# Unit 0's row maxima moved from the start of attention into the last stretch of the projection stage

## The chip, the cores and the metric

The kernel runs on one core of one Trainium2 chip. The metric is the device time of one execution in microseconds; the median of several runs is compared. In the notes below PE is TensorE, DVE is VectorE, ACT is ScalarE, POOL is GpSimd and SP is the queue that issues most DMAs.

## The reference, cut to what matters

```python
# x: (4, 2048, 256); 16 heads of 16; window 128 on each side; key 0 and query 0 see everything
x = x + attention(layernorm(x)) @ Wo.T
x = x + ffn(layernorm(x))

logits  = einsum('bhqd,bhkd->bhqk', q, k) * SCALE
logits  = where(|i - j| <= 128 or i == 0 or j == 0, logits, -inf)
out     = softmax(logits) @ v

# ffn: both matrices ternary, with one scale for each row
h = x @ (tern(w_fc) * scale).T + gate * (x @ v.T @ fast_b.T @ u.T)
y = relu(h)**2 @ (tern(w_proj) * scale).T
```

## The kernel before

The work is in three stages, each with its instructions written out for every engine; semaphores tie the engines together. A stage ends for all engines at the end of its block: the next block's first instructions start together.

**Projection** (`stage_project`). Sixteen groups of 512 rows of x are normalised, turned and multiplied into q, k and v. q and k are split into three bf16 parts (HIGH, MID, LOW; `q_parts`, `k_parts`) and stored to DRAM, v (`va`) too. ACT writes HIGH and MID, DVE the rests, POOL the LOW parts (L448). Beside that DVE prepares the weights of the third stage in small pieces, `weights.dve_part(dve, i)`, two pieces for each group; making one 128x256 piece of a matrix ternary is a pair of instructions, L1027 and L1029 (`dve_ternary`), both with two operands in SBUF.

**The projection's tail.** When the sixteenth group is through, the row of query 0, which sees all keys, is computed. The maximum over the keys is taken on DVE (L716), turned on PE (L573), reduced again and put on a diagonal (L804, L806), spread over the partitions by a product (L576, the tensor `over_bank`), added to the scores (L809, the tensor `w0`), put through Exp on ACT (L681), and multiplied with v on PE: 16 rounds n of four products (L581, one for each sequence, each in its own 32 output rows). DVE divides and picks (L817, L819), PE gathers (L585), DVE copies the row out (L823), and SP, after it has waited for all q, k and v stores (L411, L412), stores the row (L414). On DVE the rest of the weights' work lies between L809 and L817: `dve_low` and five ternary pairs.

**Attention** (`stage_attend`). 64 units (16 groups of 512 queries, times four sets of four heads) pass through a pipeline, written as steps: in step i unit i-2 has its maxima taken (L_MAX), unit i-3 has them turned and split (L_SHIFT), unit i-4 has its scores and Exp (L_SCORE), unit i-5 its sums with v. For the maxima PE makes 16 tiles of 128 queries by up to 387 keys (L1503) into four PSUM banks, DVE reads each with a mask and a maximum (L1665); PE then turns the maxima (L1483, "M"), ACT, DVE and POOL split them (L1612, L1654, L1627, L1409), SP writes them as extra rows of q, and the scores (L1527) have them subtracted. In the first steps the engines also set up what attention needs: POOL writes an identity, a gate and three 32x4128 areas of ones (L1262); ACT writes the fourth (L1593) and copies the turned weights out of PSUM (`act_w1`, `act_u`, `act_w2`); PE turns them between the tiles of unit 0; and before unit 0's scores ACT clears the score banks (L1639, semaphore `s_init`), behind unit 0's Exp at key 0 (L1631), which needs POOL's L1414. POOL's L1409 and L1414 stand behind its three areas of ones.

**Feed forward** (`stage_feed`) follows and is not touched.

The wait at the head of unit 0's scores is this:

```python
if n == 0:
    if us.n == 0:
        pe.wait_ge(s_init, 3)
    if us.n < UPG:
        pe.wait_ge(s_ones[us.hq], 1)
    pe.wait_ge(s_row[us.upar], (us.uhalf + 1) * DMA * SHIFT_ROWS)
```

## Time and profile before

| what | value |
|---|---|
| median of 3 runs | 1153.87 us (1153.65 to 1155.17) |
| profiled execution, its time | 1157.08 us |
| its span in the profile | 1155.4 us |
| granted TensorE clock, mean | 0.992 |
| PE, DVE, ACT, POOL busy | 98%, 85%, 73%, 61% of the span |
| projection with its tail | 0 to 185.05 us |
| attention | 185.05 to 781 us, the last of its sums (L1549) |
| feed forward | the rest |

The rows give a start in microseconds from the span's beginning and a duration. A row with "x8" merges eight instructions of one kind. What stands in brackets is how long the engine sat idle ahead of it and what ended that. One fp32 product appears as two records. The span is 1.7 us shorter than the profiled execution's time, and that execution was 3.2 us above the median.

### The profile page before, as it was taken

The page shows a single profiled execution, that of the slowest core. Times are in us where ns is not written, and L with a number is a line of the kernel's source. Part 1 is how long each engine was busy: PE and PEld are TensorE (multiplying, and loading weights), DVE is VectorE, ACT ScalarE, POOL GpSimd, SP SyncE. Part 2 cuts the span into 40 slices and gives each one's busy share as a digit, 9 for nine tenths or more (in the row PEclk, how much of TensorE's full clock was granted, in tenths as well). Part 3 has the DMA queues.
Part 4 walks back from the last instruction along what each step waited for, and adds up shares of the span by engine and source line. Part 5 has one row for each costly group of instructions (what it writes and reads, how often), then busy time and mean ns, then how long its engine had stood idle before and what let it go on. Part 6 is the DMA issues. An engine that isn't in the chain of part 4 may idle for free.

```text
span 1155.4 us, 26575 instructions
## 1 busy us (share of the span) xinstructions
PE 1126.5 (98%) x9115; PEld 784.2 (68%) x9115; DVE 978.4 (85%) x3169; ACT 843.7 (73%) x1513; POOL 706.7 (61%) x935
## 2 busy tenths in 40 slices
PE   8999998999999999999999999999999999999997
PEld 7888884455555555555555555558888988898886
DVE  7789857899889998899888999867888888888885
ACT  7989984788888878888888888875565556555654
POOL 3665565577788777887778877773344334433443
PEclk9999998899999999999999999999999999999999
DMA  6999997655556556555565464240231113111201
GB/s 196 287 296 276 268 235 187 120 123 130 129 132 130 129 119 139 131 119 131 129 137 132 112 138 109 69 139 28 73 107 59 56 55 107 59 55 56 74 20 37
DMA packets 158150, 145.24 MB, mean 126 GB/s; under 512 B 21548, under 2 KB 157760, under 8 KB 158016
## 3 DMA queue, kind: packets, MB, share of 16 engines
q1 hardware_dynamic: 158016, 143.54, 49.5%
q8 instruction: 73, 1.20, 0.5%
q14 instruction: 61, 0.50, 0.2%
HBM read 91.74 MB, written 50.95 MB: 124 GB/s over the span
## 4 chain that ended last, share of the span: by engine, by line
PE 72%; DVE 7%; issue 2%; ACT 1%; POOL 1%; DVEq 0%; POOLq 0%; ACTq 0%
PE e_psum L1549 15%; PE e_psum L1503 15%; PE e_psum L1527 14%; PE e_psum L1837 6%; PE e_psum L1839 5%; PE e_psum L1267 3%; PE e_psum L1818 3%; PE e_psum L1817 3%; DVE n_stats L142 2%; DVE f_x L1936 2%; PE e_psum L1822 1%; PE e_psum L255 1%; PE e_psum L254 1%; PE e_psum L253 1%; PE e_psum L1786 1%
## 5 line engine op out<-in xcount | busy, mean ns | idle before, releaser
L1665 DVE CUSTOM_DVE_ANT_0 a_masked<-e_psum,band 128x387 f32<-128x387 f32 (+1 forms) x1024 | 493.2, 534 | 59.3 <-PE e_psum L1503 56.4
L1622 ACT ACTIVATE a_weights<-e_psum 128x1024 f32<-128x1024 f32 (+1 forms) x512 | 397.9, 806 | 87.2 <-PE e_psum L1527 82.3
L1401 POOL TENSOR_SCALAR_AFFINE_SELECT a_weights<-a_weights 128x1024 f32<-128x1024 f32 x256 | 276.2, 1091 | 59.9 <-ACT a_weights L1622 58.7
L1503 PE MATMUL e_psum<-e_k,e_q 96*128 96x387 bf16 (+1 forms) x1024 | 281.2, 326 | 3.5 <-PEq L281 2.0
L1878 POOL TENSOR_TENSOR f_square<-f_relu 128x512 f32<-128x512 f32 x128 | 146.1, 1142 | 209.6 <-ACT f_relu L1867 192.2
L1527 PE MATMUL e_psum<-e_q,e_k 128*128 128x384 bf16 (+2 forms) x1408 | 255.5, 278 | 1.5 <-ACT a_weights L1622 1.1
L1549 PE MATMUL e_psum<-a_weights,a_v 128*17 128x384 f32 (+2 forms) x2816 | 195.8, 392 | 1.0 <-POOL a_weights L1401 1.0
L1527 PEld LDWEIGHTS e_psum<-e_q,e_k 128*128 128x128 bf16 x1408 | 128.9, 98 | 95.7 <-issue 39.7
L1503 PEld LDWEIGHTS e_psum<-e_k,e_q 96*128 96x128 bf16 x1024 | 100.3, 98 | 99.8 <-DVE a_max L1665 44.6
L1837 PE MATMUL e_psum<-w_w_t,f_square_hi 128*128 128x256 f32 x512 | 129.4, 287 | 5.6 <-DVE f_square_lo L1924 5.6
L1839 PE MATMUL e_psum<-w_w_t,f_square_lo 128*128 128x256 f32 x512 | 126.7, 282 | 0.0
L1867 ACT ACTIVATE f_relu<-e_psum,w_mag 128x512 f32<-128x512 f32 x128 | 87.2, 681 | 52.7 <-PE e_psum L1822 52.7
L1924 DVE TENSOR_TENSOR f_square_lo<-f_square,f_square_hi 128x512 fp32r<-128x512 f32 x128 | 98.5, 789 | 24.2 <-POOL f_square L1878 24.2
L1549 PEld LDWEIGHTS e_psum<-a_weights,a_v 128*17 128x17 f32 x2816 | 61.6, 96 | 67.5 <-issue 53.7
L1837 PEld LDWEIGHTS e_psum<-w_w_t,f_square_hi 128*128 128x128 f32 x512 | 96.6, 189 | 15.1 <-DVE f_square_lo L1924 12.1
L1817 PE MATMUL e_psum<-f_xt_hi,w_w_t 128*128 128x512 f32 x256 | 102.7, 401 | 1.1 <-ACT f_relu L1867 1.1
L1818 PE MATMUL e_psum<-f_xt_lo,w_w_t 128*128 128x512 f32 x256 | 101.2, 395 | 0.0
L1839 PEld LDWEIGHTS e_psum<-w_w_t,f_square_lo 128*128 128x128 f32 x512 | 96.9, 189 | 2.9
L1870 ACT ACTIVATE f_square_hi<-f_relu 128x512 fp32r<-128x512 f32 x128 | 81.0, 633 | 4.1
L448 POOL TENSOR_TENSOR p_q_parts<-p_rest,p_q_parts 128x512 bf16<-128x512 f32 x32 | 38.3, 1196 | 71.2 <-ACT p_q_parts L613 71.2
L1665 DVE DVE_READ_ACCUMULATOR2_ANT a_max<- 128x1 f32 x1024 | 78.8, 77 | 0.0
L1860 ACT ACTIVATE f_z<-e_psum 128x512 fp32r<-128x512 f32 x16 | 9.6, 597 | 90.1 <-PE e_psum L1809 90.1
(217 smaller groups left out, 2057.0 us busy)
## 6 DMA issues: line engine op xcount, KB each, us to landing
k_parts<-p_k_parts SPq DMA_DIRECT2D x48, 258.0 KB, 5.2
e_k<-k_parts SPq DMA_DIRECT2D x64, 193.5 KB, 3.8
e_k<-k_parts SPq DMA_DIRECT2D x192, 64.5 KB, 3.4
q_parts<-p_q_parts SPq DMA_DIRECT2D x48, 256.0 KB, 5.7
e_q<-q_parts SPq DMA_DIRECT2D x64, 192.0 KB, 3.9
e_q<-q_parts SPq DMA_DIRECT2D x192, 64.0 KB, 3.4
v_ones<-p_va SPq DMA_DIRECT2D x16, 544.0 KB, 6.4
p_x<-in_x SPq DMA_DIRECT2D x16, 512.0 KB, 7.4
```

The source lines that it names most:

```text
L1401: pool.affine_select(out=blocks, in_=blocks, compare_op=ALU.is_ge, fill=0.0, base=0, pattern=[[0, NQ // 2 * HEAD_COLS // P // CUT_STEP], [ ...
L1503: pe.matmul(sh.tile_bank(ux, j)[:, lo:hi], qw[ux.q][0:SLOT_ROWS, h, t * P:t * P + P], kt[ux.hq][0:SLOT_ROWS, h, start + lo:start + hi], st ...
L1527: ins = pe.matmul(score[third // 2][:, c0:c0 + m * P], kt[us.hq][:, h, k0:k0 + P], qw[us.q][:, h, qb * P:(qb + m) * P], start=True, stop=True)
L1549: ins = pe.matmul(sum_bank[32 * j:32 * j + VW, qb * P:(qb + m) * P], vw[:, up.gpar, kb + 1, h * VW:h * VW + VW], pe_w[:, up.upar, c0:c0 + ...
L1622: act.activation(pe_w[:, us.upar, lo:hi], score[c % 2][:], ACT.Exp).then_inc(s_exp, 1)
L1665: dve.tensor_tensor_reduce(out=masked[:, ux.upar, h, t:t + hi - lo], in0=bank[:, lo:hi], in1=band[:, lo:hi], scale=1.0, scalar=NEG, op0=AL ...
L1817: pe.matmul(self.h_bank[j % 2][:], lhs, self.sh.xt_hi[:, q.par, k, :], start=(k == 0), stop=False)
L1818: pe.matmul(self.h_bank[j % 2][:], lhs, self.sh.xt_lo[:, q.par, k, :], start=False, stop=False)
L1837: pe.matmul(y, sh.r2_hi[:, j % 4, part], self.w.w2_t[:, j, :], start=(j == 0 and t == 0), stop=False, skip_group_check=True)
L1839: ins = pe.matmul(y, sh.r2_lo[:, j % 4, part], self.w.w2_t[:, j, :], start=False, stop=(j == MH - 1), skip_group_check=True)
L1878: pool.tensor_tensor(sh.r2[:, j % 4, :], sh.r[:, j % 4, :], sh.r[:, j % 4, :], ALU.mult).then_inc(self.s_sq, 1)
L1924: dve.tensor_tensor(sh.r2_lo[:, j % 4, :], sh.r2[:, j % 4, :], sh.r2_hi[:, j % 4, :].bitcast(F32), ALU.subtract).then_inc(self.s_r2lo, 1)
```

## The change

- `sh.pe_first_tile` and `sh.dve_first_tile`: the 16 tiles and maxima of unit 0 are made in the projection's tail. They use three banks in turn. On PE tiles 0 and 1 stand behind L576, tiles 2 to 4 behind the wait for `w0`, and tiles 5 to 15 one each between the rounds of query 0's sums. On DVE tile 0 stands ahead of `w0`, the others behind it. The masked values are written over the q parts of the even groups, so DVE waits for their stores.
- `dve_part`: all eight ternary pairs of `w_proj` now stand in the last three groups (three, three and two, where there was one each), the filling of `v_t` in an earlier group; the five pairs in the tail are gone.
- ACT issues the loads of q of units 2 and 3 in the tail, behind Exp; SP no longer issues them in attention (their k it still does).
- Attention begins with the maxima of unit 1. The turning of the weights on PE stands between unit 1's tiles, and ACT's first copies stand behind unit 0's MID. The identity is kept from the first stage; POOL no longer writes it again.
- POOL writes the mask band (`pool_band`) in group 5 and not in the tail.

```diff
@@ stage_project, SP
             sp.wait_ge(s_v, G * TB)
-            for n in range(1, PRELOADED):
-                sh.load_unit(sp, Unit(n), q_dram, k_dram)
+            sh.load_unit(sp, Unit(1), q_dram, k_dram)
@@ stage_project, POOL
+                    if q.g == GB + 1:
+                        sh.pool_band(pool)
 
             sweep(body, LP)
-            sh.pool_band(pool)
-            pool.wait_ge(sh.s_band, 2)
             pool.wait_ge(s_v, G * TB)
+            pool.wait_ge(s_gap, G * KT)
             sh.pool_zeros(pool)
@@ stage_project, PE
             pe.matmul(over_bank[:, 0:B * H], ones[0:B * H, :], m_diag[:], start=True, stop=True).then_inc(s_rpe, 1)
-            idle_products(total_bank, 10)
+
+            sh.pe_first_tile(pe, 0)
+            sh.pe_first_tile(pe, 1)
+            idle_products(sum_bank, 4)
+            pe.wait_ge(s_rv, 4)
+            for j in range(2, 5):
+                sh.pe_first_tile(pe, j)
             pe.wait_ge(s_rexp, 1)
             for n in range(NB):
                 for b in range(B):
                     ins = pe.matmul(sum_bank[QR * b:QR * b + H, 0:VROW], w0[:, b, n, :], v_of[:, b, n, 0:VROW],
                                     start=(n == 0), stop=(n == NB - 1))
+                if n + 5 < TILES:
+                    sh.pe_first_tile(pe, n + 5)
             ins.then_inc(s_rpe, 1)
@@ stage_project, ACT
+
+            act.wait_ge(s_v, G * TB)
+            for n in range(PRELOADED, Q_PRELOADED):
+                sh.load_q(act, Unit(n), q_dram)
@@ stage_project, DVE
+            dve.wait_ge(s_qout[0], DMA * STORES * (G // 2))
+            sh.dve_first_tile(dve, 0, masked)
             dve.wait_ge(s_rpe, 2)
             for b in range(B):
                 ins = dve.tensor_tensor(w0[:, b], s0_of[:, b],
                                         over_bank[:, b * H:(b + 1) * H].unsqueeze(1).broadcast_to([P, NB, H]), ALU.add)
             ins.then_inc(s_rv, 1)
+            for j in range(1, TILES):
+                sh.dve_first_tile(dve, j, masked)
             weights.dve_low(dve)
-            for n in range((2 * G - weights.TERN2) // 2, 4 * KT):
-                weights.dve_ternary2(dve, n)
+            dve.wait_ge(sh.s_tile_read, TILES)
+            dve.tensor_copy(sh.first_key0[:].rearrange("p (c r) -> p r c", r=3), masked[:, :, 0:TILES // 3 + 1])
             dve.wait_ge(s_rpe, 3)
@@ Weights.dve_part
-        elif i >= self.TERN2 and i % 2 == 0:
-            self.dve_ternary2(dve, (i - self.TERN2) // 2)
+        elif i >= self.TERN2:
+
+            for n in ((0, 1), (2,), (3, 4), (5,), (6,), (7,))[i - self.TERN2]:
+                self.dve_ternary2(dve, n)
@@ Shared
+    def pe_first_tile(self, pe, j):
+
+        if j == 0:
+            pe.wait_ge(self.s_load[0], self.loaded(Unit(0)))
+        if j >= 3:
+            pe.wait_ge(self.s_tile_read, j - 2)
+        t, h = divmod(j, NQ)
+        start, lo, hi = self.keys_of(0, t)
+        pe.matmul(self.first_bank(j)[:, lo:hi], self.qw[0][0:SLOT_ROWS, h, t * P:t * P + P],
+                  self.kt[0][0:SLOT_ROWS, h, start + lo:start + hi], start=True, stop=True).then_inc(self.s_tile, 1)
@@ stage_attend, SP
                 if (u := at(0)) and u.n >= PRELOADED:
                     wait(sp, s_score, (u.n - Q_BUFS) * CHUNKS + CHUNKS)
-                    sh.load_unit(sp, u, q_dram, k_dram)
+                    sh.load_k(sp, u, k_dram)
+                    if u.n >= Q_PRELOADED:
+                        sh.load_q(sp, u, q_dram)
@@ stage_attend, POOL
-            identity(pool, ident[:], s_ident)
@@ stage_attend, PE
-                    if not ux:
+                    if not ux or ux.n == 0:
                         return
...
-                    if ux and ux.n == 0 and j in (1, 3):
-                        pe.wait_ge(s_ident, 2)
+                    if ux and ux.n == 1 and j in (1, 3):
                         weights.pe_w1(pe, 2 + j // 2)
...
-                    if ux and ux.n == 1 and j == 3:
+                    if ux and ux.n == 1 and j == TILES - 1:
                         weights.pe_mag(pe)
```

In the tail of the projection, PE's rows before are these; L576 spreads the maxima, L487 are ten products that nobody reads, L581 are the sums of query 0, and attention begins behind the branches:

```order
L573 MATMUL p_bank<-p_ident,p_m_tok 64x128
L1077 MATMUL p_bank<-p_ident,z_w_in 128x128 x4
L576 MATMUL p_bank<-p_m_diag,p_ones 128x64
L487 MATMUL p_bank<-p_ones 128x128 x10
L581 MATMUL p_bank<-p_va,p_w 16x272 x64
L585 MATMUL p_bank<-p_picked,p_seq_of 4x272
L281 UNCONDITIONAL_BRANCH
L1457 UNCONDITIONAL_BRANCH
L1503 MATMUL e_psum<-e_k,e_q 128x258 x2
```

And these are PE's rows there now; L580 is the old L576, L1297 is `pe_first_tile`, and L591 is the old L581:

```order
L580 MATMUL p_bank<-p_m_diag,p_ones 128x64
L1297 MATMUL e_psum<-e_k,e_q 128x258 x2
L491 MATMUL p_bank<-p_ones 128x128 x4
L1297 MATMUL e_psum<-e_k,e_q 128x258 x2
L1297 MATMUL e_psum<-e_k,e_q 128x387
L591 MATMUL p_bank<-p_va,p_w 16x272 x4
L1297 MATMUL e_psum<-e_k,e_q 128x387
L591 MATMUL p_bank<-p_va,p_w 16x272 x4
L1297 MATMUL e_psum<-e_k,e_q 128x387
...
L1297 MATMUL e_psum<-e_k,e_q 128x387
L591 MATMUL p_bank<-p_va,p_w 16x272 x20
L597 MATMUL p_bank<-p_picked,p_seq_of 4x272
```

Where 64 products of the sums stood in one piece, eleven tiles now stand between the first eleven rounds of four; the last five rounds follow in one piece.

On DVE, the last group of the projection and what follows it before the change, from the last ternary pair of the group (L1027, L1029) to `w0` (L809):

```order
L733 TENSOR_TENSOR p_rest<-p_bank,p_k_parts 128x512 x2
L1027 TENSOR_TENSOR z_below<-z_w_in,z_nhalf 128x256
L1029 SCALAR_TENSOR_TENSOR z_w_in<-z_w_in,z_half,z_below 128x256
L716 TENSOR_REDUCE p_m_tok<-p_va 128x16
L804 TENSOR_REDUCE p_m_neg<-p_bank 64x1
L806 TENSOR_SCALAR p_m_diag<-p_ident,p_m_neg 64x64
L809 TENSOR_TENSOR p_w<-p_va,p_bank 128x256 x4
```

And the same place now, where L732 is the maximum over the keys, L1307 is `dve_first_tile` and L828 is `w0`:

```order
L1054 TENSOR_TENSOR z_below<-z_w_in,z_nhalf 128x256
L1056 SCALAR_TENSOR_TENSOR z_w_in<-z_w_in,z_half,z_below 128x256
L1054 TENSOR_TENSOR z_below<-z_w_in,z_nhalf 128x256
L1056 SCALAR_TENSOR_TENSOR z_w_in<-z_w_in,z_half,z_below 128x256
L732 TENSOR_REDUCE p_m_tok<-p_va 128x16
L820 TENSOR_REDUCE p_m_neg<-p_bank 64x1
L822 TENSOR_SCALAR p_m_diag<-ident,p_m_neg 64x64
L1307 ISA p_q_parts,first_max<-e_psum,band 128x258
L1307 ISA first_max 128x1
L828 TENSOR_TENSOR p_w<-p_va,p_bank 128x256 x4
```

A second ternary pair stands ahead of the maximum over the keys, and unit 0's first tile ahead of `w0`.

On POOL, the start of attention before, with its four small setup instructions and the three areas of ones, ahead of the LOW split of unit 0's maxima:

```order
L106 MEMSET e_ident 128x128
L108 AFFINE_SELECT e_ident<-e_ident 128x128
L1385 MEMSET a_gate 128x16
L1387 AFFINE_SELECT a_gate<-a_gate 128x16
L1262 MEMSET e_k 32x4128 x3
L1409 TENSOR_TENSOR a_shift<-a_neg_rest,a_shift 16x128
L1414 TENSOR_TENSOR a_d<-a_masked,a_max 128x16
```

And now:

```order
L1448 MEMSET a_gate 128x16
L1450 AFFINE_SELECT a_gate<-a_gate 128x16
L1326 MEMSET e_k 32x4128 x3
L1472 TENSOR_TENSOR a_shift<-a_neg_rest,a_shift 16x128
L1477 TENSOR_TENSOR a_d<-first_key,first_max 128x16
```

The identity is gone from the head; the areas of ones still stand between the block's start and unit 0's LOW.

## Rows read from the trace of the kernel before

**Rows 1.** The page's costliest groups: busy us, mean ns of one | idle before, releaser.

```profile
L1665 DVE CUSTOM_DVE_ANT_0 a_masked<-e_psum,band 128x387 f32<-128x387 f32 (+1 forms) x1024 | 493.2, 534 | 59.3 <-PE e_psum L1503 56.4
```

**Rows 2.** Windows of 25.6 us: busy time by engine, clock, DMA share, GB/s.

```profile
179.20:204.80 25.60, 19.08 (x126) 11.48 (x119) 18.51 (x76) 11.42 (x17) 11.87 (x9) 0.82 0.76 168
```

**Rows 3.** The final chain, 150 to 260 us: start, duration, what.

```profile
194.35 0.29 PE e_psum L1483
...
203.66 0.38 PE e_psum L1483
```

**Rows 4.** Timeline of the projection's tail: start, duration, engine, line, operands.

```profile
168.88 0.61 DVE L716 TENSOR_REDUCE p_m_tok<-p_va 128x16 f32<-128x256 f32 x1 [1.43 <-ACT p_va L618]
...
170.34 0.64 DVE L806 TENSOR_SCALAR p_m_diag<-p_ident,p_m_neg 64x64 f32<-64x64 f32 x1
...
171.03 0.43 PE L576 MATMUL p_bank<-p_m_diag,p_ones 64*128 64x64 f32 x2 [0.61 <-DVE p_m_diag L806]
...
171.50 1.41 DVE L809 TENSOR_TENSOR p_w<-p_va,p_bank 128x256 f32<-128x256 f32 x4 [0.53 <-PE p_bank L576]
...
174.06 7.53 PE L581 MATMUL p_bank<-p_va,p_w 128*16 128x272 f32 x128 [0.16 <-ACT p_w L681]
...
175.60 0.68 DVE L1051 TENSOR_TENSOR w_wo_lo<-p_bank,w_wo_hi 128x512 fp32r<-128x512 f32 x1
...
183.14 0.41 DVE L823 COPY row<-p_bank 4x256 f32<-4x256 f32 x1 [0.71 <-PE p_bank L585]
...
184.25 0.26 SPq L414 DMA_DIRECT2D attention<-row  x1
185.05 0.55 SPq L1228 DMA_DIRECT2D e_k<-k_parts  x1
```

**Rows 5.** Timeline of the first steps of attention.

```profile
185.56 0.11 POOL L1385 MEMSET a_gate<- 128x16 f32 x1
...
186.02 10.50 POOL L1262 MEMSET e_k<- 32x4128 f32 x3
...
193.24 0.60 ACT L1122 ACTIVATE w_w_t<-e_psum 128x512 fp32r<-128x512 f32 x1 [0.34 <-PE e_psum L1094]
...
198.12 2.06 ACT L1639 ACTIVATE e_psum<-e_ident 128x1024 f32<-128x1024 f32 x3
...
203.83 1.06 PE L1527 MATMUL e_psum<-e_q,e_k 128*128 128x384 bf16 x4
```

**Rows 6.** Timeline of DVE and POOL, a ternary pair and LOW parts in two groups.

```profile
130.37 0.89 DVE L1027 TENSOR_TENSOR z_below<-z_w_in,z_nhalf 128x256 f32<-128x256 f32 x1
130.94 1.31 POOL L448 TENSOR_TENSOR p_k_parts<-p_rest,p_k_parts 128x512 bf16<-128x512 f32 x1
131.30 1.24 DVE L1029 SCALAR_TENSOR_TENSOR z_w_in<-z_w_in,z_half,z_below 128x256 f32<-128x256 f32 x1
...
166.51 0.41 DVE L1027 TENSOR_TENSOR z_below<-z_w_in,z_nhalf 128x256 f32<-128x256 f32 x1
166.96 0.48 DVE L1029 SCALAR_TENSOR_TENSOR z_w_in<-z_w_in,z_half,z_below 128x256 f32<-128x256 f32 x1
...
168.44 1.12 POOL L448 TENSOR_TENSOR p_k_parts<-p_rest,p_k_parts 128x512 bf16<-128x512 f32 x1
```

**Rows 7.** The final chain in attention, sums between other products.

```profile
218.34 0.77 PE e_psum L1549 x8
219.10 0.27 PE e_psum L1503
...
219.60 0.17 PE e_psum L1503
```

**Rows 8.** DMA issues from 174 to 182 us, and a wait of SP.

```profile
v_ones<-p_va SPq DMA_DIRECT2D x1, 544.0 KB, 10.1
...
e_q<-q_parts SPq DMA_DIRECT2D x1, 192.0 KB, 7.0
...
SPq L412 <- DMA v_ones<-p_va: 0.9, 1, 0.9
```

More of the change, by code:

```diff
@@ L1132, with __init__ @@
 class Shared:
-    def __init__(self, nc, outer, ctx, row, band, weights_words):
+    def __init__(self, nc, outer, ctx, row, band, ident, first, weights_words):
         def sb(name, shape, dt=F32):
@@ L1148, in sem @@
             return outer.enter_context(nc.semaphore(f"e_{name}"))
-        self.nc, self.row, self.band = nc, row, band
+        self.nc, self.row, self.band, self.ident = nc, row, band, ident
+        self.first_key0, self.first_max = first
         with ExitStack() as place:
@@ L2067, in layer @@
         band = outer.enter_context(nc.sbuf_tensor("band", [P, -(-WINDOW // 16) * 16], BF16))
+        ident = outer.enter_context(nc.sbuf_tensor("ident", [P, P], F32))
+        first = [outer.enter_context(nc.sbuf_tensor(f"first_{name}", shape, F32))
+                 for name, shape in (("key0", [P, TILES + 2]), ("max", [P, TILES]))]
         with ExitStack() as place:
             weights = Weights(nc, outer, wo, fast_b, w_fc, w_proj, u, v, gate)
-            sh = Shared(nc, outer, place, row, band, Weights.WORDS)
+            sh = Shared(nc, outer, place, row, band, ident, first, Weights.WORDS)
         stage_project(nc, x, (wq, wk, wv), q_dram, k_dram, va_dram, o_dram, weights, sh)
```

105 lines of the change are left out of this document (65 added, 40 removed).

## The prediction

> **What bounds the kernel now.** The final chain runs through PE's products in nearly all of attention and feed forward, so work that is moved can give time back only where PE is not full. I read the windows for such a stretch: it is the seam between projection and attention: from 179.20 to 204.80 PE is busy for 19.08 of 25.6 us, at a granted clock of 0.82 of full speed [rows 2]. The seam has three pieces. The tail is a chain through DVE, PE and ACT from the maximum over the keys at 168.88 to the row's store at 184.25, with 7.53 us of sums on PE as its longest link [rows 4]. Attention starts at 185.05 [rows 4]. Its first unit's maxima are turned at 194.35 and the second's at 203.66 [rows 3]: each time 16 tiles that DVE reads at 0.53 us each [rows 1]. At 203.83 PE starts on unit 0's scores [rows 5], 18.78 us after attention began. The question is how much of these 18.78 us falls away, and what the tail pays for it.
>
> **What attention gives back.** The plain count is 194.35 - 185.05 = 9.3 us, all of unit 0's maxima [rows 3, 4]. But unit 0's scores wait for two things. The second is a chain that begins with the block on POOL: the gate's setup (185.56), three areas of ones (186.02, 10.50 us), then LOW and key 0's difference, then ACT's Exp, the weights' magnitudes and the clearing of the score banks (198.12, 2.06 us, so to 200.18) [rows 5]. Before the change it ends 3.65 us ahead of 203.83 and costs nothing. It stays in the new kernel, shorter by the identity only. The gate's first instruction will stand at the block's start, so the chain takes 200.18 - 185.56 = 14.62 us, and with 0.05 for PE to see it the scores start 14.7 us into attention. Gain: 18.78 - 14.7 = **4.1 us**, not 9.3. ACT's first copies, moved behind unit 0's MID, ended at 193.84, 8.8 us into the block [rows 5]; now they begin about 1.6 us later and end at about 10, beneath POOL's memsets. Unit 1's tiles with the weights between them take what unit 0's took, some 10 us, and are covered too; if that cover were gone, each microsecond past 14.7 would be paid. Unit 1's turned maxima and unit 2's first tile are then ready when the scores start. This, and a clock that may rise earlier than it did, I put at **0.3 us**, between 0 and 1.2.
>
> **What the tail pays.**
>
> *Ternary pairs.* Two stand where one stood in the last group. The first keeps its 166.51 and 166.96 and ends at 167.44 [rows 6]; but a pair that meets POOL's LOW parts took 0.89 and 1.24 us, with the 1.24 lasting beyond POOL's 1.31 [rows 6]. In the last group the second pair runs into LOW parts too, one of them at 168.44 [rows 6], so it costs 2.17 us (130.37 to 132.54 [rows 6]) to twice 1.24. I take 2.5: it ends at 169.95 and the maximum over the keys starts 1.07 us late. Some comes back at L806: its 0.64 us for 64x64 ended with a LOW part, which will be over by then; I estimate 0.3. PE's spreading product moves from 171.03 by **+0.8** (0 if the pairs don't meet, +2 if L806 meets the first memset of q's rows instead). The Trainium skill, "SBUF — State Buffer", section "SBUF: two separate sides", says that a DVE instruction with two SBUF inputs and a GpSimd instruction that reads SBUF exclude each other for whole instructions. By it the second pair can only run between two LOW parts, as the slow rows show; without it this term would be 0 and the total 0.8 us less. The pairs moved into the two groups before may make DVE's next rests a microsecond or two late, but the banks that these free are wanted by PE only a group later, and DVE catches up in its waits for ACT (1.43 us even in the last group [rows 4]): nothing is paid there. The filling of `v_t` is hidden likewise.
>
> *Tile 0 ahead of `w0`.* DVE now waits for one product more and reads one tile, 0.53 us [rows 1], less what it waited anyway: **+0.5**. Exp and the sums start 1.3 us late, at about 175.4.
>
> *Eleven tiles between the rounds.* 128 records of sums in 7.53 us [rows 4] are 16 rounds at 0.47, in which four products run at once in their own rows. A tile needs the whole array. The trace has this pattern in attention: eight records of 384 columns in 0.77 us, and the tile after them shows 0.27 where others show 0.17 [rows 7]. Together 0.87, where the tail's pace would give 384/272 x 0.47 = 0.66: breaking a piece costs 0.21. Each inserted tile so costs 0.17 + 0.21 = 0.38, eleven of them **+4.2**. The bounds are 11 x 0.17 = 1.9 (nothing for breaking) and 5.5 (0.5 each, were weight loads bare as well).
>
> *DVE's end.* Tile 15's product comes behind round 11, at 175.4 + 11 x 0.85 = 184.7, and is read by 185.5; then comes `dve_low`, which lay between 172.91 and 176.28, 3.4 us with the filling of `v_t` [rows 4]; I take 2.0 for what is left with the copy of key 0's column (1.5 to 3.4). DVE is ready at 187.5, PE's sums at 187.1: **+0.4**.
>
> *The end.* Before, the row's copy ended at 183.55, but SP stored it at 184.25 [rows 4], since it waited 0.9 us for the last store of v, which took 10.1 us to land [rows 8]. The new q loads on ACT's queue, 8 DMAs and 0.77 MB, share the same DMA engines; at the 168 GB/s of that window [rows 2] they delay that landing by at most 4.6 us, from 184.0 to 188.6. The copy now ends at 183.55 + 0.8 + 0.5 + 4.2 + 0.4 = 189.45, after it. So SP's wait is gone: **-0.6**.
>
> The tail grows by 0.8 + 0.5 + 4.2 + 0.4 - 0.6 = 5.3 us, and attention starts at about 190.35.
>
> **Sum.** +5.3 - 4.1 - 0.3 = **+0.9 us**. The profiled execution would go from 1157.1 to 1158.0, the median from 1153.87 to 1154.8. From 0.2% (2.3 us) on a measurement of this kernel can tell a difference; this is no change.
>
> **Rivals.**
> 1. *The breaks are free* (0.17 a tile). The sums end 2.3 us earlier, but then DMA binds: with v landing at 187 to 188.6 attention starts near 188.2, 3.1 us late and not 5.3. Total -1.3; with the early clock's 1.2 in place of 0.3 it is -2.2: 1151.7 to 1152.6. For it: bf16 and fp32 products follow each other elsewhere without a gap. Against it: rows 7. 20%, of which a quarter beyond 0.2%.
> 2. *POOL's chain does not hold the scores*, so that the full 9.3 us come back: +5.3 - 9.3 = -4.0, 1149.9. It would need the memsets to be shorter than 10.50 us, or LOW's wait to matter less. Against it: they stand ahead of L1409 in the order, and their length is in the row. 10%.
> 3. *Slower.* The breaks cost more than the attention rows show. The total is 11p - 3.3 for a price of p per tile; at 0.38 it is +0.9 and from p = 0.51 it passes 2.3 us. For it: bare weight loads of 128 columns before and 16 behind each tile. Against: the rows already contain such a change. At the bound of 0.5 with L806's +1.2 it is +3.4, 1157.3. 16%.
> 4. *Unit 1's loads come late.* Its last q load, issued up to 181.8, landed 7.0 us later [rows 8]; 3 to 4.6 us more is 191.8 to 193.4, where attention starts at 190.35. POOL's cover takes about 2 us of that; it decides beyond 193.8, when it would add 1.4 us: 1156.3 or more. 9%.
>
> **Chances and range.** The forecast has 45%. Within 0.2%: 45 + 15 (most of rival 1) = 60%; faster 15% (rivals 1's rest and 2); slower 25% (rivals 3 and 4). The terms' bounds give 1152 (free breaks, early clock) to 1157.3 (L806 blocked, dear breaks); that leaves out rival 2 and little of 3.
>
> **What the profile after will show.** Right: scores of unit 0 start 14.7 us behind the first instruction of attention, with PE idle before them and released through ACT's clearing; attention starts near 190.3; L591 spans about 11.9 us with DVE never the later one in its first rounds; the maximum over the keys starts near 170; SP waits for the row and not for v. Wrong: L591 under 10.5 us or over 13, the second pair at 0.9 us, attention's start held by a DMA, or scores earlier than 14 us. An effect beyond the seam, in feed forward or in steady steps, would not be mine at all.

## Result, and the profile after

The changed kernel takes 1157.63 us against 1153.59 us, medians of 13 runs each; the ratio is 1.0028 with a 95% interval of 1.0021 to 1.0035, so it is **slower by 0.28%, 3.2 us** (2.4 to 4.0). One run of the changed kernel was disturbed (6185.91 us) and does not count in the ratio. The two medians alone lie 4.0 us apart, which is the upper end of the interval. I had forecast +0.9 us and no change that a measurement could tell. Its profiled execution took 1157.63 us, its span was 1155.9 us. That is 0.5 us more than the first profile of the kernel before, so the two profiles alone seem to bear my forecast out. The rest of this text is about the 2.7 us between these two statements.

The tail on VectorE: two ternary pairs of the last group, then the maximum over the keys, the exponents' argument, and the end (start, duration, engine, line, operands, and the idle time with what ended it).

```profile
165.62 0.41 DVE L1054 TENSOR_TENSOR z_below<-z_w_in,z_nhalf 128x256 f32<-128x256 f32 x1
...
166.66 1.21 DVE L1054 TENSOR_TENSOR z_below<-z_w_in,z_nhalf 128x256 f32<-128x256 f32 x1
167.90 1.23 DVE L1056 SCALAR_TENSOR_TENSOR z_w_in<-z_w_in,z_half,z_below 128x256 f32<-128x256 f32 x1
169.06 0.60 DVE L732 TENSOR_REDUCE p_m_tok<-p_va 128x16 f32<-128x256 f32 x1
...
171.89 1.41 DVE L828 TENSOR_TENSOR p_w<-p_va,p_bank 128x256 f32<-128x256 f32 x4
...
186.38 0.17 DVE L838 RECIPROCAL p_rden<-p_bank 128x1 f32<-128x1 f32 x1 [0.25 <-PE p_bank L591]
```

The first pair starts at 165.62, where it was 166.51 in [rows 6]: the whole projection ran 0.89 us earlier in this execution, so every distance below is counted from this pair. The second pair takes 1.21 and 1.23 us instead of 0.41 and 0.48. POOL's LOW parts lie over it:

```profile
166.13 1.45 POOL L451 TENSOR_TENSOR p_q_parts<-p_rest,p_q_parts 128x512 bf16<-128x512 f32 x1 [0.78 <-ACT p_q_parts L625]
167.55 1.30 POOL L451 TENSOR_TENSOR p_k_parts<-p_rest,p_k_parts 128x512 bf16<-128x512 f32 x1
```

Each of the pair's two instructions ends 0.3 us behind the end of a LOW part (167.87 behind 167.58, 169.13 behind 168.85). The maximum over the keys starts 3.44 us behind the first pair, before it was 2.37 [rows 4, 6]: +1.07, the predicted size. Ahead of the reciprocal VectorE sat idle for 0.25 us, waiting for TensorE's sums, so its own work was done before them. TensorE in the same stretch, with the unit 0 tiles that now stand between the rounds, and its start into attention:

```profile
170.71 0.43 PE L580 MATMUL p_bank<-p_m_diag,p_ones 64*128 64x64 f32 x2 [0.26 <-DVE p_m_diag L822]
...
174.44 0.65 PE L591 MATMUL p_bank<-p_va,p_w 128*16 128x272 f32 x8 [0.41 <-ACT p_w L693]
175.03 0.34 PE L1297 MATMUL e_psum<-e_k,e_q 96*128 96x387 bf16 x1
175.29 0.65 PE L591 MATMUL p_bank<-p_va,p_w 128*16 128x272 f32 x8
...
183.83 2.49 PE L591 MATMUL p_bank<-p_va,p_w 128*16 128x272 f32 x40
...
199.55 0.28 PE L1547 MATMUL e_psum<-ident,a_max 128*16 128x128 f32 x1
203.86 1.03 PE L1591 MATMUL e_psum<-e_q,e_k 128*128 128x384 bf16 x4 [4.03 <-ACT e_psum L1704]
```

A round with its tile takes 0.85 us (174.44 to 175.29), and the last five rounds stand together in 2.49 us. The sums last from 174.44 to 186.32, 11.88 us as against 7.53 in [rows 4]. SyncE now waits for the row alone: the last store of v, which I had feared would land up to 4.6 us later, landed 8.6 us after its issue, where it had been 10.1 [rows 8]. SyncE starts attention at 189.18:

```profile
188.38 0.26 SPq L417 DMA_DIRECT2D attention<-row  x1
189.18 0.55 SPq L1248 DMA_DIRECT2D e_k<-k_parts  x1
```

Attention starts 23.56 us behind the pair; before, 18.54 (185.05 - 166.51). The tail grew by 5.0 us; I had said 5.3. POOL and ACT in the first step of attention:

```profile
189.64 10.49 POOL L1326 MEMSET e_k<- 32x4128 f32 x3
```

```profile
191.28 3.64 ACT L1656 ACTIVATE e_k<-ident 32x4128 f32<-32x4128 f32 x1
...
201.01 0.21 ACT L1696 ACTIVATE e_p<-a_d 128x16 f32<-128x16 f32 x1 [1.75 <-POOL a_d L1477]
...
201.74 2.06 ACT L1704 ACTIVATE e_psum<-ident 128x1024 f32<-128x1024 f32 x3
```

ACT waits 1.75 us for POOL's differences, then clears the score banks for 2.06 us, and TensorE starts the scores at 203.86, having idled 4.03 us: 14.68 us behind the block's start, predicted 14.7. The second unit's maxima are turned at 199.55, well before. So the costs of the tail and the wait that starts the scores stand where I had put them.

### The profile page after: what moved, and what is told of

The parts are those of the page before. It is cut to its first block, busy times and chain, and to the rows that moved or that the text cites. A ratio compares the mean times of both kernels' runs of the same rounds, so it can differ in the third digit from the quotient of the medians.

```text
span 1155.9 us, 26551 instructions
## 1 busy us (share of the span) xinstructions
PE 1124.8 (97%) x9103; PEld 780.8 (68%) x9103; DVE 985.6 (85%) x3170; ACT 844.3 (73%) x1513; POOL 707.1 (61%) x933
## 4 chain that ended last, share of the span: by engine, by line
PE 72%; DVE 6%; issue 2%; ACT 1%; POOL 1%; DVEq 0%; POOLq 0%; ACTq 0%
PE e_psum L1613 15%; PE e_psum L1567 15%; PE e_psum L1591 14%; PE e_psum L1902 6%; PE e_psum L1904 5%; PE e_psum L1331 3%; PE e_psum L1883 3%; PE e_psum L1882 3%; DVE n_stats L144 2%; DVE f_x L2001 2%; PE e_psum L1887 1%; PE e_psum L255 1%; PE e_psum L257 1%; PE e_psum L256 1%; PE e_psum L1851 1%
## 5 line engine op out<-in xcount | busy, mean ns | idle before, releaser
L1730 DVE CUSTOM_DVE_ANT_0 a_masked<-e_psum,band 128x387 f32<-128x387 f32 (+1 forms) x1008 | 486.3, 534 | 60.9 <-PE e_psum L1567 56.3
L1567 PE MATMUL e_psum<-e_k,e_q 96*128 96x387 bf16 (+1 forms) x1008 | 276.2, 326 | 1.9 <-DMA e_q<-q_parts 1.9
```

Source lines behind the costliest of these rows:

```text
L1567: pe.matmul(sh.tile_bank(ux, j)[:, lo:hi], qw[ux.q][0:SLOT_ROWS, h, t * P:t * P + P], kt[ux.hq][0:SLOT_ROWS, h, start + lo:start + hi], st ...
L1730: dve.tensor_tensor_reduce(out=masked[:, ux.upar, h, t:t + hi - lo], in0=bank[:, lo:hi], in1=band[:, lo:hi], scale=1.0, scalar=NEG, op0=AL ...
```

## Experiments

All were made to find where the 2.7 us are. A ratio is always that to the kernel before, with its 95% interval; the number after each kernel's name in the table tells how far its one profiled execution lies above (+) or below (-) the median of the timed runs of that kernel taken beside it. Four distances take the whole seam apart; each is the difference of two rows of one profile. "Pair" is the first ternary pair of the last group, "block" SyncE's first load in attention, "scores" TensorE's first score product, "maxima" ACT's reading of the turned maxima of unit 3, which is the third reading if the one beside the first scores is counted.

| kernel (profiled execution against median, us) | pair to block | block to scores | scores to maxima | maxima to end |
|---|---|---|---|---|
| before, first profile (+3.5) | 18.54 | 18.78 | 18.41 | 933.16 |
| before, second (-0.2) | 17.95 | 17.35 | 18.15 | 933.15 |
| before, third (-0.9) | 17.95 | 17.35 | 18.74 | 933.15 |
| changed (0.0) | 23.56 | 14.68 | 18.82 | 933.22 |
| POOL's fill later (-0.6) | 23.52 | 14.28 | 16.91 | 933.19 |
| tiles in groups (-1.3) | 21.92 | 14.69 | 17.85 | 933.30 |
| ternary pair earlier (+1.7) | 24.09 | 14.68 | 17.98 | 933.24 |
| q of 2 and 3 by SyncE in attention (+3.1) | 24.97 | 14.68 | 22.10 | 933.18 |
| changed, idle products at three places (+1.1) | 28.05 | 16.90 | 16.91 | 933.25 |
| before, idle products at three places (+0.4) | 19.86 | 24.27 | 16.91 | 933.19 |
| 10 idle products (0.0) | 23.49 | 14.70 | 17.07 | 933.25 |
| three edits (-0.8) | 21.08 | 14.33 | 17.72 | 933.18 |
| three edits, SyncE loads q (+0.8) | 22.75 | 12.64 | 17.94 | 933.68 |
| six edits (-0.2) | 21.87 | 11.89 | 17.49 | 933.24 |

The last column is the same within 0.15 us, but for one 0.5: behind the seam nothing happened. (It is worked out from spans given to 0.1 us, so its second figure says nothing.) The pair itself started between 164.09 and 166.51 in all profiles, of the old kernel and of the new ones alike. In the four kernels with the second pair one group earlier (the ternary pair alone, three edits, and the two built on them) the last group's pair starts 0.28 us later against the group before it (8.92 us behind that group's first pair instead of 8.65), so 0.28 us have to be added to their first column before it is compared with the others.

**1. The kernel before, profiled again.** No edit.

> The kernel before, unchanged, profiled a second time. Its profiled execution stood 3.5 us above the median of its timed ones (1157.08 against 1153.59), so the rows that I compared the change with may not be those of a usual execution. Theory A (the change costs the 5.0 us that its tail grew by and gets back the 4.1 us of the earlier scores; what is missing lies in the old profile): this execution has its span near 1152 us, and differs from the first profile of before at a place that I can name: in the projection loop (the first pair of the last group at 165.6 us or less instead of 166.5) or around the first scores (half clock from 202 to 209 us shorter than there). Theory B (the change pays something more after 215 us that I have not seen): the span is again near 1155 us and every stage of it stands as in the first profile, so that the 3 us between the medians must come from the changed kernel.

It took 1153.54 us with a span of 1151.7. SyncE at the end of the tail and the start of attention:

```profile
182.24 0.26 SPq L414 DMA_DIRECT2D attention<-row  x1
183.05 0.55 SPq L1228 DMA_DIRECT2D e_k<-k_parts  x1
```

and VectorE at the pair and at the row's copy:

```profile
165.10 0.42 DVE L1027 TENSOR_TENSOR z_below<-z_w_in,z_nhalf 128x256 f32<-128x256 f32 x1
...
181.73 0.41 DVE L823 COPY row<-p_bank 4x256 f32<-4x256 f32 x1 [0.71 <-PE p_bank L585]
```

The row's copy ended 17.04 us behind the pair in both profiles (here 181.73 + 0.41 - 165.10, in the first 183.14 + 0.41 - 166.51), but SyncE stored it 0.10 us later here and 0.70 us later in the first [rows 4]. What SyncE waited for here, in its list of waits, was the row, and not the store of v, for which it had waited 0.9 us in the first profile [rows 8]:

```profile
SPq L413 <- DVE row L823: 0.3, 1, 0.3
```

TensorE, at the weights' magnitudes, the second turn of maxima and the scores:

```profile
192.99 1.11 PE L1103 MATMUL e_psum<-z_mag_diag,p_ones 128*128 128x128 f32 x8
...
200.22 0.38 PE L1483 MATMUL e_psum<-e_ident,a_max 128*16 128x128 f32 x1 [0.97 <-DVE a_max L1665]
200.40 1.06 PE L1527 MATMUL e_psum<-e_q,e_k 128*128 128x384 bf16 x4
```

The scores start 17.35 us behind the block, where the first profile has 18.78. The windows of the clock say why. Of this profile (columns: window and its length, busy us and instructions of TensorE, its weight loads, VectorE, ACT and POOL; granted clock, DMA share, GB/s):

```profile
184.00:186.00 2.00, 2.00 (x18) 1.72 (x17) 1.81 (x9) 2.00 (x1) 1.98 (x1) 1.00 0.71 167
186.00:188.00 2.00, 0.86 (x7) 0.45 (x5) 2.00 (x9) 1.98 (x3) 2.00 (x2) 1.00 0.79 173
...
194.00:196.00 2.00, 1.54 (x8) 0.52 (x6) 1.70 (x7) 0.60 (x2) 1.11 (x3) 1.00 0.01 2
...
200.00:202.00 2.00, 1.78 (x9) 1.19 (x9) 1.08 (x6) 0.78 (x2) 0.00 (x0) 0.50 1.17 219
```

and of the first:

```profile
184.00:186.00 2.00, 0.81 (x4) 0.46 (x5) 0.48 (x3) 0.35 (x1) 0.78 (x4) 0.81 1.12 238
186.00:188.00 2.00, 2.00 (x11) 1.81 (x10) 1.08 (x6) 2.00 (x1) 1.98 (x1) 0.50 0.90 196
...
196.00:198.00 2.00, 2.00 (x10) 1.56 (x10) 0.54 (x3) 0.61 (x2) 1.11 (x3) 0.50 0.03 4
```

In the first profile the clock is at half (1.2 GHz) in the block's first microseconds and again around 196, here it is full (2.4 GHz) in both and falls only at the scores. The eight records of the magnitudes take 1.11 us here and took 1.95 there, and VectorE waited 1.46 us for a tile behind them there. Theory A holds, at both of its places. Of the 3.6 us between the two spans 1.41 lie ahead of the pair (166.51 against 165.10), where the clock is full in both profiles and I have no cause, 0.59 in the tail, 1.43 between block and scores and 0.26 behind them. How unusual the first profile is, the timed executions of the kernel before tell: of 84 on record none took longer than 1156.33 us, and it took 1157.08. **The third profile** repeats the second:

> The kernel before, unchanged, profiled a third time. Theory A: the distance from the last group's first ternary pair to the block is 18.5 us (second profile 18.46; the first, with clock at half from 184.8 to 188.5 us, 19.05), and from the block to the scores 16.8 us (second 16.84, first 18.27), unless its own row of clocks shows a stretch at half inside them; the third transpose of maxima then lies 933.2 us ahead of the end as in every profile so far. Rival (18.27 is as usual as 16.84): it comes out near 18.3 with no clock row to blame.

This expectation (and that of experiment 6 for the old kernel) counts the block from POOL's gate (L1385), 0.51 us behind SyncE's first load, so its 18.46 and 16.84 are the 17.95 and 17.35 of the table.

```profile
182.06 0.55 SPq L1228 DMA_DIRECT2D e_k<-k_parts  x1
```

```profile
199.41 1.06 PE L1527 MATMUL e_psum<-e_q,e_k 128*128 128x384 bf16 x4
```

1153.03 us, span 1151.3; again 17.95 and 17.35 us, to the hundredth, and no window under full clock from 166 to 198 us. What it adds is a longer half clock behind the scores (18.74 us for 18.15). Theory B, a cost elsewhere in the changed kernel, falls with the last column of the table.

**2. POOL's fill of the ones rows later.**

```diff
-            for q in range(1, UPG):
-                sh.ones_filled(pool, q)
...
                                        ).then_inc(s_d0, 1)
+                    if um.n == 0:
+                        pool.wait_ge(s_d0, 1)
+                        for q in range(1, UPG):
+                            sh.ones_filled(pool, q)
```

> The changed kernel, with POOL's filling of the ones rows of keys 1, 2 and 3 (the 10.49 us of memsets) put behind its two operations for unit 0 (the low part of the maxima and the differences to key 0) instead of ahead of them. In the changed kernel ACT waited 1.75 us for those differences and the scores began 14.68 us after the block. Theory A (POOL's queue binds there, as I forecast): the scores begin 1.75 us earlier, 12.9 us after the block start, bound by ACT's own copies, and the ratio to the kernel before falls by 1.75 us plus what a shorter idle TensorE gives back in clock: 1.0010 to 1.0015 instead of 1.0028. Rival (the start of the scores doesn't set the end, since the 2.06 us of ACT's zeroing or SP's rows come last, or the memsets now hold up POOL's first cuts): ratio stays at 1.0028 within 0.0005.

Ratio 1.0007 (0.9998 to 1.0016), 2.4 us under the changed kernel's. The gain was had another way than I expected: the scores moved by 0.4 us only, and in the profiled execution 1.9 us came behind them, where the clock now stayed full. POOL had stopped to bind, but a stretch at half clock lay in TensorE's transposes of weights, for which ACT's copies wait:

```profile
194.94 1.06 PE L1118 MATMUL e_psum<-ident,z_w_in 128*128 128x128 f32 x4
...
201.90 0.61 PE L1593 MATMUL e_psum<-e_q,e_k 128*128 128x384 bf16 x4 [2.56 <-ACT e_psum L1706]
```

```profile
196.04 0.60 ACT L1146 ACTIVATE w_w_t<-e_psum 128x512 fp32r<-128x512 f32 x1 [0.60 <-PE e_psum L1118]
197.49 0.60 ACT L1146 ACTIVATE w_w_t<-e_psum 128x512 fp32r<-128x512 f32 x1 [0.85 <-PE e_psum L1118]
```

Four transposes take 1.06 us here and 0.60 at full clock.

The kernel with three edits and SyncE's q loads has the same change and no half clock there: 12.64 us, where I had 12.9. So POOL's queue binds at 14.68, and 12.64 was measured with it out of the way.

**3. The eleven tiles in groups.**

```diff
-                if n + 5 < TILES:
-                    sh.pe_first_tile(pe, n + 5)
+                for j in {2: (5, 6, 7), 5: (8, 9, 10), 8: (11, 12, 13), 10: (14, 15)}.get(n, ()):
+                    sh.pe_first_tile(pe, j)
```

> The changed kernel, with the eleven tiles that stand singly between query 0's sums put there in three groups of three and one of two, after the third, sixth, ninth and eleventh round: the same 11 products and 11 maxima with 4 breaks instead of 11. In the changed kernel a round with its tile took 0.853 us against 0.47 without (7.53 us for 16 rounds), 0.17 of it the tile. Theory A (the break costs, 0.21 us each): the sums take 11.9 - 7 x 0.21 = 10.4 us, and the time falls by 1.5 us: ratio 1.0015. Rival (the 0.38 us belong to the tile itself, its weight load and its columns, whoever stands beside it): sums stay at 11.7 to 11.9 us, ratio 1.0028. Second rival: three tiles in a row wait for VectorE's reading of the tile three before, which adds 0.3 to 0.6 us a group and gives the gain away.

```profile
172.97 1.57 PE L591 MATMUL p_bank<-p_va,p_w 128*16 128x272 f32 x24 [0.40 <-ACT p_w L693]
174.47 0.67 PE L1297 MATMUL e_psum<-e_k,e_q 96*128 96x387 bf16 x3
175.06 1.57 PE L591 MATMUL p_bank<-p_va,p_w 128*16 128x272 f32 x24
```

Ratio 1.0012 (1.0003 to 1.0021). Three rounds and three tiles take 2.09 us (172.97 to 175.06) where singly they took 3 x 0.853 = 2.56 (0.853 is the mean of eleven rounds, 174.44 to 183.83): two breaks fewer, 0.24 us each. The tail is 1.64 us shorter, expected 1.5. The price of a break is shown, and VectorE's reading holds nothing up: TensorE has no idle time between the groups. This profiled execution was the fastest of its eleven timed runs, 1.3 us below their median, so its row may flatter it.

**4. The second ternary pair one group earlier.**

```diff
-            for n in ((0, 1), (2,), (3, 4), (5,), (6,), (7,))[i - self.TERN2]:
+            for n in ((0, 1), (2,), (3, 4), (5, 6), (7,), ())[i - self.TERN2]:
```

> The changed kernel, with the second ternary pair of the last group made one group earlier, so that the last group has one pair as in the kernel before, and the group ahead of it four pairs instead of three. In the changed kernel that second pair ran beside POOL's low parts at 1.21 and 1.23 us instead of 0.41 and 0.48 and the maxima over the keys began 1.07 us later against the loop. Theory A: the maxima begin 1.07 us earlier, everything to the attention block with them, the ratio falls by 0.9 us, to 1.0020. Rival (the fourth pair a group earlier makes VectorE late for the last group's remainders, by 1.7 us, and the maxima start as late as before): ratio 1.0028 or up to 1.0035.

```profile
166.51 0.62 DVE L732 TENSOR_REDUCE p_m_tok<-p_va 128x16 f32<-128x256 f32 x1 [0.38 <-ACT p_va L630]
```

The maximum over the keys starts 2.10 us behind the pair (164.41) instead of 3.44. Of these 1.34 us 0.28 are the pair's own later start, so 1.07 are gained, as expected. The ratio is 1.0020 (1.0011 to 1.0029), also as expected, but its interval and that of the changed kernel overlap, so the times alone don't tell the two apart. This profiled execution was the slowest of its eleven timed runs, 1.7 us above their median, and its tail is 0.5 us longer than the changed kernel's, since its first rounds of sums ran at half clock:

```profile
173.18 0.96 PE L591 MATMUL p_bank<-p_va,p_w 128*16 128x272 f32 x8
...
174.50 1.11 PE L591 MATMUL p_bank<-p_va,p_w 128*16 128x272 f32 x8
...
177.21 0.65 PE L591 MATMUL p_bank<-p_va,p_w 128*16 128x272 f32 x8
```

A round with its tile took 1.32 us there (173.18 to 174.50); a round's eight records took 0.96 us and from 177.21 on 0.65 again. Three of the ten profiles with the new order have such a stretch at 172 to 179 us (the others are the changed kernel with idle products at three places and that with q by SyncE in attention), and none of the four with the old order. The change took six of ten idle products from ahead of the sums; that this is the reason was not tried.

**5. Queries of units 2 and 3 loaded by SyncE in attention, as before.** The constant `Q_PRELOADED` is 2 instead of 4.

> The changed kernel with the queries of units 2 and 3 loaded by SP in the attention block, as before, instead of by ACT in the tail. I took this part at nothing. Theory A: ratio 1.0028 within 0.0004. Rival (the eight early transfers lie beside unit 1's load and hold it up: in the changed kernel TensorE's first tile of unit 1 waited 1.86 us for that load, some 0.5 us beyond the block's start): the first tile starts 0.5 us earlier, and where the clock allows the scores too: ratio 1.0024. Opposite rival (SP's queue becomes longer again, and the rows of maxima for the first scores go out later): ratio 1.0030 to 1.0040.

Ratio 1.0045 (1.0031 to 1.0058). TensorE, 9.65 us behind the first scores:

```profile
214.37 0.28 PE L1567 MATMUL e_psum<-e_k,e_q 96*128 96x258 bf16 x1 [1.84 <-DMA e_q<-q_parts]
```

It waits 1.84 us for unit 3's queries, and behind that wait the clock falls to half for 6 us:

```profile
218.00:220.00 2.00, 2.00 (x11) 0.18 (x10) 1.22 (x6) 1.02 (x1) 0.34 (x1) 0.50 0.85 169
```

The readings of maxima at 214.80 and 226.82 lie 12.02 us apart, against 8.84 in the changed kernel. I had this part at nothing. The intervals of the two ratios overlap a little, and this profiled execution lies 3.1 us above the median of its own six timed runs, so the size in time is uncertain; the stall is in the rows of this one execution. With the scores 2.7 us nearer to the block, loads that were on time in the old order are late, and the early loads are what hides that; this reading is argued from the one stall.

**6. Idle products, too many.** Six behind the sums, ten behind the total, and ahead of the first scores (`WARM` is 24):

```diff
                         if us.n == 0:
+                            bank_read(TURN_OF_TILE[1])
+                            for _ in range(WARM):
+                                pe.matmul(sh.tile_bank(ux, 1)[:, 0:P], ident[:], ident[:], start=True, stop=True)
                             pe.wait_ge(s_init, 3)
```

> The changed kernel with idle 128x128 products on TensorE where it had nothing to do: 6 behind query 0's sums, 10 behind the total, and 24 (about 2.7 us) ahead of the first scores, where it waited 4.0 us for ACT. In the changed kernel's profile the granted clock fell to half at 189.8 us for some 3 us and at 203.2 us for some 7 us, and from the scores' start to the third transpose of maxima it took 18.82 us, against 16.91 us in the kernel whose POOL fill stands later, which had full clock there. Theory A (this half clock behind idle stretches is a part of the time at this seam, and differs from execution to execution): the clock stays at 1.00 behind the first scores, that distance comes down to 16.9 to 17.0 us, and the time falls by 1.5 to 2.0 us, ratio about 1.0013. Rival (the half clock is hidden under ACT and VectorE, which pace these steps): ratio 1.0028 within 0.0005, though the clock is full.

> The kernel before with the same idle products at the same three places. Its second profile has the clock at half from 199 to 205 us, and 18.15 us from the scores' start to the third transpose of maxima; the first profile has also 184.8 to 188.5 and 194 to 198.4 us at half, and 18.27 us from the block's start to the scores against 16.84. Theory A: ratio 0.9985 to 0.9990 (1.2 us from the stretch behind the scores, and fewer executions with the second one), and a narrower spread of its times than the 1152.6 to 1156.3 us of the kernel before. Rival (no stretch on the path): ratio 1.0000, or above it by up to 0.0005 since the 24 products can end after ACT's zeroing.

```profile
203.69 5.52 PE L1585 MATMUL e_psum<-ident 128*128 128x128 f32 x48
209.04 0.60 PE L1598 MATMUL e_psum<-e_q,e_k 128*128 128x384 bf16 x4
```

1.0051 (1.0036 to 1.0066) and 1.0057 (1.0044 to 1.0071): my count was wrong by a factor of two, for an fp32 product is two records, and the 24 took 5.52 us in the changed kernel and 7.15 in the old one, where the clock was at half for a part of them (0.50 in the window 202 to 204). Nor were they the only cost. The ten behind the total ran until 183.77 in the old kernel, and its block came 1.9 us later than without them (19.86 for 17.95 us); in the changed kernel the block came 4.5 us later (28.05 for 23.56), with a stretch at half clock in the sums. So these two ratios don't price the 24 alone. The clock behind the 24 was full, and scores to maxima took 16.91 us in both.

**7. Ten idle products**, ahead of the first scores alone.

> The changed kernel with 10 idle products ahead of the first scores and none elsewhere. In the run with 24 of them they took 5.52 us (0.23 us each, not the 0.11 that I had counted), longer than the 4.0 us gap, so that its scores began 2.3 us later than ACT's zeroing allowed; but from the scores' start to the third transpose of maxima it took 16.91 us, in both kernels with such products, against 18.82 us in the changed kernel. Now 2.3 us of products lie inside a gap of 4.0 us. Theory A (the half clock behind the gap is on the path and an idle engine brings it): scores 14.7 us after the block's start as in the changed kernel, 16.9 us to the third transpose, ratio 1.0028 - 0.0016 = 1.0012. Rival (the clock still falls, since 1.7 us of idle time stay, or because of what TensorE did earlier): distance 18 to 18.8 us, ratio 1.0028.

```profile
203.28 0.61 PE L1596 MATMUL e_psum<-e_q,e_k 128*128 128x384 bf16 x4 [1.47 <-ACT e_psum L1709]
```

Ratio 1.0017 (1.0008 to 1.0026), expected 1.0012. The scores start 14.70 us behind the block, unmoved, and it is 17.07 us to the maxima instead of 18.82. Four score products took 0.61 us, where they took 1.03 in the changed kernel: the clock is full there. All four profiles with products ahead of the first scores have it full from the scores on (with 5, 10 or 24 of them); of the ten without, nine have it at half there, and only the one with POOL's fill later does not. The half clock behind the gap is on the path, for up to 1.9 us in a profile, and idle time of TensorE ahead of the scores goes with it. The gain in the ratio, 0.0011, is 1.3 us, but the two intervals overlap (1.0021 to 1.0026), so its size is uncertain.

**8. Three edits together** (2, 3 and 4).

> The changed kernel with all three edits of the first runs together: POOL's fill behind its operations for unit 0, the eleven tiles in four groups, the second ternary pair of the last group one group earlier. Alone they took 2.1, 1.6 and 0.8 us off the ratio (1.0007, 1.0012, 1.0020 against 1.0028). If they add up: 1.0028 - 0.0021 - 0.0016 - 0.0008 = 0.9983, under the kernel before. If the first two gained in part from the same thing (both had fewer half-clock microseconds behind the scores): 0.9990 to 0.9995. The tail from the last group's first ternary pair to the block should be 23.5 - 1.6 - 1.3 = 20.6 us, and the scores 14.3 us or less behind the block's start.

```profile
187.19 0.40 PE L1569 MATMUL e_psum<-e_k,e_q 96*128 96x258 bf16 x1 [3.08 <-DMA e_q<-q_parts]
```

Ratio 0.9996 (0.9987 to 1.0004). The sum of the three would be 0.9983; with the four intervals that go into that sum the times alone can't tell the two apart, but the rows show a part of what is missing. The tail is 2.5 us shorter (2.2 with the pair's later start), but attention now starts so early that TensorE stands for unit 1's queries: my fourth rival, late loads. In the changed kernel the same wait ends 0.5 us behind the block's start and lies under POOL's queue.

**9. The same, with the early q loads behind unit 1's on SyncE.**

```diff
-            for n in range(PRELOADED, Q_PRELOADED):
-                sh.load_q(act, Unit(n), q_dram)
...
             sh.load_unit(sp, Unit(1), q_dram, k_dram)
+            for n in range(PRELOADED, Q_PRELOADED):
+                sh.load_q(sp, Unit(n), q_dram)
```

> The kernel with the three edits together, and the queries of units 2 and 3 loaded by SP behind unit 1's load instead of by ACT ahead of it. In the kernel with the three edits the tail came down to 21.07 us as it should, but TensorE's first tile of unit 1 waited 3.08 us for its queries, issued 178.67 to 180.8 us and landed at 187.1, and the scores began 14.34 us after the block: half of the tail's gain was lost again. Theory A (the eight transfers of 1.5 MB on ACT's queue, issued 171.2 to 177.3 us, lie ahead of unit 1's in the busy DMA engines): unit 1's load lands 1 to 2 us earlier, the scores with it, and the ratio falls from 0.9996 to 0.9982 to 0.9990. Rival (SP's issue order and the stores ahead of it set the landing, not the other queue): landing and ratio as they were, 0.9996.

```profile
178.96 2.76 SPq L1249 DMA_DIRECT2D e_q<-q_parts  x3
...
184.51 1.53 SPq L1249 DMA_DIRECT2D e_q<-q_parts  x3
186.30 0.26 SPq L419 DMA_DIRECT2D attention<-row  x1
```

Ratio 0.9993 (0.9984 to 1.0002), no gain that can be told. Unit 1's load lands sooner (the list of DMA issues has a median of 3.4 us to landing for the three large loads of queries, where unit 1's had 6.7), and TensorE no longer waits for it. But SyncE is issuing until 186.04 and stores the row at 186.30, though its copy ended at 184.54. Behind the pair the block starts 1.7 us later, and the scores stand 35.39 us behind the pair as against 35.41: one wait took the other's place.

**10. Six edits: the same, with the clearing split and five idle products.**

```diff
-                            pe.wait_ge(s_init, 3)
+                            pe.wait_ge(s_init, 1)
...
+                    if n == 2 and us.n == 0:
+                        pe.wait_ge(s_init, 2)
```

The sums wait for the third, and the idle products stand where the 24 stood.

> The kernel of the run beside it, and two more edits at the first scores: TensorE waits for the zeroing of the first score bank pair alone (1.03 us of ACT's 2.06), for the others where it first writes them, and 5 idle products stand in the gap. Expected against the run beside it: scores 1.0 us earlier, 13.0 us or less after the block's start, and 16.9 us to the third transpose instead of 17.7: ratio 0.0010 to 0.0016 lower, 0.9970 to 0.9980, which would be clearly below the kernel before. Rival (with the zeroing split the rows of maxima from SP come last): gain of 0.3 us or less.

```profile
199.17 0.61 PE L1599 MATMUL e_psum<-e_q,e_k 128*128 128x384 bf16 x4
```

Ratio 0.9984 (0.9975 to 0.9993): 1.8 us faster than the kernel before, 5 us faster than the change. I had hoped for 0.9970 to 0.9980; the scores came 0.75 us earlier, the stretch behind them was 0.45 us shorter. Against the kernel of experiment 9 the ratio is lower by 0.0009, with overlapping intervals; what each of the last two edits gave was not taken apart.

## Where the prediction was right and where it was wrong

The measured +3.2 us lie inside the stated range, whose upper end (1157.3, +3.4 us) was worked out from L806 blocked and dear breaks. Neither happened, so that end held by luck. The sum of +0.9 us was 2.3 us too small, and by my own line of 0.2% the change is slower, which I had given 25%.

The mechanisms of the tail and of the scores' start held, and the sum for the profiled execution nearly so: predicted +0.9 us, and from the pair to the end it is 990.28 us against 988.89, +1.4. **The step that failed is the last of the sum**, "the profiled execution would go from 1157.1 to 1158.0, the median from 1153.87 to 1154.8". I moved a difference from one execution, 3.2 us above the median, to the median, without asking whether what is slow in it lies inside the terms of the sum. It did: 2.0 us sat in two of them. The usual execution is here that of the second and third profile, whose times (1153.54 and 1153.03 us) lie within 0.9 us of the median and whose distances up to the scores agree to the hundredth:

- *"Gain: 18.78 - 14.7 = 4.1 us".* The 14.7 was right (14.68). The 18.78 held 1.43 us of half clock in the first step of attention. In the usual execution it is 17.35, and the gain **2.67 us**. The row for the suspicion was in my own hands: a clock of 0.82 from 179.20 to 204.80 [rows 2]. I took it as a chance of a gain, not as a cost that a usual execution of the old kernel doesn't pay.
- *"SP's wait is gone: -0.6".* In the usual execution that wait isn't there (0.10 us from the copy to the row's store in both later profiles): **0**.

The others:

- Ternary pairs, +0.8: measured +0.57 (TensorE's spreading product 5.09 us behind the pair, before 4.52). What DVE and POOL do to each other was right: 1.21 and 1.23 us with POOL's parts over the pair, 0.41 and 0.48 without. By the Trainium skill, "SBUF — State Buffer", section "SBUF: two separate sides", a DVE instruction with two SBUF inputs and a GpSimd instruction that reads SBUF exclude each other for whole instructions; this trace agrees, with each slow instruction ending 0.3 us behind a LOW part.
- Tile 0 ahead of `w0`, +0.5: +0.71.
- Eleven tiles, +4.2: 11.88 - 7.53 = **+4.35**, 0.40 each; experiment 3 shows the break in it at 0.24 where I had 0.21.
- DVE's end, +0.4: 0, the reciprocal waited 0.25 us for TensorE.
- The early maxima and the clock behind the scores, -0.3: scores to maxima 18.82 against 18.15 and 18.74, so **+0.1 to +0.7**. A longer idle time ahead of the scores bought no earlier clock; experiment 7 speaks for a cost.

With the usual execution the sum is 0.57 + 0.71 + 4.35 - 2.67 + (0.1 to 0.7) = **+3.1 to +3.7 us**, and 3.2 (2.4 to 4.0) were measured. This rests on one profile of the changed kernel, whose time is its median, and two of the kernel before. Rival 3, slower, had the right sign and the wrong cause: the tiles cost what I had said. Rival 2 fell (the scores waited for POOL's chain, 14.68 us), rival 1 too (a break costs 0.24 us). Rival 4 came to life only when the tail was shortened. Queries of units 2 and 3, which I gave no term, seem worth a stall: without their early loads the ratio was 1.0045.

What stays open: why the first profile had its half clock where it was, why its loop ended 1.4 to 2.4 us later than in the other two, and whether the stretch in the changed kernel's sums, in three of ten profiles of the new order, comes from the idle products that were taken out. Its share in the medians can't be read from single profiles.

## What to carry to other kernels

Before a difference is read from one profile, set its time beside the median: here 3.2 us lay between them, as much as the effect, and 2.0 us of it sat in the very stretches that the change removed. A second profile of the unchanged kernel would have shown it. The same holds for the profiles of experiments: here they lay between 1.3 us below and 3.1 us above their own medians. And where work is moved to let the next stage begin sooner, look at each thing that stage waits for: POOL's queue took 2 us of the gain, the loads took the next where POOL no longer did, and each was hidden by what had been slower.

## What was unexpected of the hardware

- TensorE's clock fell to half (1.2 GHz) at the seam (172 to 223 us) in all 14 profiles, and otherwise only in the last 5 us of each, but at other places in other executions of one and the same program: at 186, 196 and 204 us in the first profile of the kernel before, only from 199 us in the second and third. The Trainium skill, "TensorE: Matmul & The Clock Gate", section "Part 1: The HAM clock gate (the "warmup" mystery)", says that the counting which decides it runs free and isn't set back by a kernel's start, so that the turning point varies from run to run. That the places vary, these three profiles show; that this is the reason, and why whole stretches were missing from two of them, no run here shows. The half clock was worth 1.4 us ahead of the scores and up to 1.9 behind them.
- A break between sums in four groups of output rows and one product over the whole array costs 0.24 us, more than the product itself (0.17).
